# Masked cross attention on one core: masks as one 128-row product per bank, and a work order of its own

## What is computed

```python
def _L1_xattn_ref(q, k, v, mask, Wq, bq, Wk, bk, Wv, bv, Wo, bo):
    ...
    scale = 1.0 / jnp.sqrt(jnp.float32(dh))
    scores = jnp.einsum('hbsd,hbtd->hbst', qh, kh) * scale
    scores = jnp.where(mask == 0, jnp.float32(-1000000000.0), scores)
    attn = jax.nn.softmax(scores, axis=-1)
    out = jnp.einsum('hbst,hbtd->hbsd', attn, vh)
    out = out.transpose(1, 2, 0, 3).reshape(b, s, d)
    return out @ Wo.T + bo
x = x + jnp.tanh(g_xattn[1]) * _L1_xattn_ref(_layernorm(x, axis=-1), ctx_1024, ctx_1024, mask_SxS2_ik0, ...)
```

## Time and profile before

| what | us |
|---|---|
| median of 3 runs | 3282.59 |
| lowest, highest | 3279.39, 3283.39 |
| the profiled execution's own time | 3312.22 |
| its span, first to last instruction | 3310.4 |
| TensorE busy, share of the span | 2888.8 (87%) |
| VectorE busy | 2030.2 (61%) |
| ScalarE busy | 1995.5 (60%) |
| GpSimd busy | 1581.2 (48%) |
| granted TensorE clock, mean | 0.927 |

### The profile page before, as it was taken

How to read it: one execution, slowest core, us unless ns; L and a number is a source line. 1 busy time by engine, 2 the same in 40 slices (tenths; PEclk the granted TensorE clock), 3 DMA queues, 4 the chain that set the end, 5 groups by cost and what they waited for, 6 DMA issues and landing times. The chain is left out here.

```text
span 3310.4 us, 76280 instructions
## 1 busy us (share of the span) xinstructions
PE 2888.8 (87%) x27986; PEld 1847.8 (56%) x27986; DVE 2030.2 (61%) x3872; ACT 1995.5 (60%) x5960; POOL 1581.2 (48%) x1845
## 2 busy tenths in 40 slices
PE   4896998899889988998899879987999988996896
PEld 1554776467647664666477647763555543552452
DVE  3665886588658865886588758874333323665573
ACT  3345887588758885888488848883122233455343
POOL 0524885488638863887288728870311100420430
PEclk8798999999999999999999999999588899899798
DMA  2001001000010001000100010001000000000000
GB/s 92 1 2 45 16 18 40 17 18 18 20 36 18 18 15 42 18 18 15 41 17 18 16 40 18 18 16 53 1 1 1 1 1 0 1 2 0 1 2 13
DMA packets 35866, 60.31 MB, mean 18 GB/s; under 512 B 7184, under 2 KB 32656, under 8 KB 33552
## 3 DMA queue, kind: packets, MB, share of 16 engines
q1 hardware_dynamic: 35472, 55.15, 5.2%
HBM read 28.91 MB, written 1.05 MB: 9 GB/s over the span
## 5 line engine op out<-in xcount | busy, mean ns | idle before, releaser
L994 POOL TENSOR_TENSOR l_qk<-l_ta,l_tb 128x256 f32<-128x256 f32 x768 | 539.9, 735 | 113.4 <-DVE l_tb L1048 113.4
L617 POOL TENSOR_SCALAR qmr<-q_all,cf 128x256 fp32r<-128x256 f32 x128 | 116.0, 925 | 847.6 <-SPq L447 410.8
L649 DVE TENSOR_REDUCE mrow<-ring 128x2 f32<-128x512 f32 x512 | 328.2, 684 | 304.6 <-PE ring L491 290.8
L1010 POOL TENSOR_TENSOR l_qk<-l_qk,l_rn 128x512 f32<-128x512 f32 x384 | 392.7, 1044 | 217.0 <-DVE l_rn L1070 217.0
L602 ACT ACTIVATE pt<-st 128x512 f32<-128x512 f32 x384 | 210.6, 599 | 423.5 <-PE st L519 423.5
L915 ACT ACTIVATE l_pr<-st,l_mn 128x128 f32<-128x128 f32 x1152 | 407.5, 382 | 38.1 <-DVE l_mn L1036 38.1
L1001 POOL TENSOR_TENSOR l_pr<-l_pr,l_rs 128x512 f32<-128x512 f32 x384 | 391.9, 1043 | 42.5 <-DVE l_rs L1060 42.5
L1052 DVE TENSOR_REDUCE l_n<-l_sq 128x8 f32<-128x512 f32 x384 | 262.8, 686 | 177.8 <-ACT l_sq L924 175.6
L513 PE MATMUL st<-qm,k_all 32*128 32x512 f32 x1024 | 338.0, 691 | 0.0
L491 PE MATMUL ring<-ktr,qmr 32*128 32x256 f32 x1024 | 246.2, 403 | 14.3 <-POOL qmr L617 11.8
L915 ACT ACTIVATION_READ_ACCUMULATOR l_pr<-st,l_mn 128x1 f32 x1152 | 255.1, 221 | 0.0
(11 more groups left out here) (237 smaller groups left out, 6795.0 us busy)
## 6 DMA issues: line engine op xcount, KB each, us to landing
l_vm<-l_v SPq DMA_DIRECT2D x192, 96.0 KB, 2.0
l_wa<-in_wa SPq DMA_DIRECT2D x7, 2048.0 KB, 9.1
l_vm<-l_v SPq DMA_DIRECT2D x192, 32.0 KB, 1.9
l_wf<-in_wf SPq DMA_DIRECT2D x6, 580.5 KB, 4.6
w<-in_w SPq DMA_DIRECT2D x1, 2752.0 KB, 15.5
cf<-in_cf SPq DMA_DIRECT2D x1, 1253.0 KB, 7.4
x<-in_xT SPq DMA_DIRECT2D x1, 1024.0 KB, 4.8
ctxT<-in_ctxT SPq DMA_DIRECT2D x1, 1024.0 KB, 9.4
```

Of the source, the lines that this page charges most:

```text
L649: dve.tensor_reduce(mrow[b % 2][:, t, j, 2 * p:2 * p + 2], bank_of(f"R{r}").rearrange("p (h k) -> p h k", h=2), AX.X, ALU.max).then_inc(ri ...
L994: ins = pool.tensor_tensor(halves[0][:, :, x], halves[1][:, :, x], halves[2][:, :, 1 - x], ALU.add)
L1010: pool.tensor_tensor(part, part, t.rn[:, :, 4 * x:4 * x + 4].unsqueeze(3).broadcast_to([P, 2, 4, LHD]), ALU.mult).then_inc(qk_normed, 1)
```

## The change

- The mask is held as `mask2_q` and `mask2_k`: 128 mask rows on 128 partitions, two tiles of them, a quarter of the bytes. `add_mask` is one product of all 128 rows with the unit matrix over the 512 columns of a bank. The table of shifted unit matrices goes away.
- An item of scores is split in three: open (waits for its bank and, in the masked layer, adds the mask), add (the products of 32 rows), and for S subtract the maxima.
- Items of S and R that follow each other in the period form a run. In the masked layer a run first opens all its items, then adds all, then subtracts the maxima of all its S. In the other layers each item is a part of its own, in the old order.
- The masked layer has an order of its own, `MASKED_PERIOD`: four runs of four S with two or three R, four runs of one or two R, and between them the value quarters in pairs. Q0 to Q7 are in the batch itself, q8 to q15 in the next. Its first 20 row items go in runs of three.
- The ring plan is made for each layer's period.

```diff
-def project(g, l, q_all, k_all, mask4, tmp):
+def project(g, l, q_all, k_all, mask2, tmp):
...
-        ints = [tmp(n, [P, 4, 2, SEQ], I32) for n in ("mask_q", "mask_k")] if l == 1 else []
+        ints = [tmp(n, [P, 2, SEQ], I32) for n in ("mask_q", "mask_k")] if l == 1 else []
...
-                    for src, dst in zip(ints, mask4):
-                        dve.tensor_scalar(dst[:, :, :, :], src[:, :, :, :], 0.0, MASKED, ALU.is_equal, ALU.mult)
+                    for src, dst in zip(ints, mask2):
+                        dve.tensor_scalar(dst[:, :, :], src[:, :, :], 0.0, MASKED, ALU.is_equal, ALU.mult)
...
 PERIOD = ("q4 q5 q6 q7 R0 R1 S0 R2 S1 S2 S3 q8 R3 R4 q9 q10 q11 S4 S5 R5 R6 R7 S6 S7 q12 q13 q14 q15 V S8 R8 R9 "
           "S9 S10 S11 R10 Q0 Q1 R11 R12 Q2 Q3 O T S12 R13 S13 S14 S15 R14 R15").split()
+MASKED_PERIOD = ("S0 S1 S2 S3 R0 R1 R2 q8 q9 R3 q10 q11 S4 S5 S6 S7 R4 R5 R6 q12 q13 R7 q14 q15 V "
+                 "S8 S9 S10 S11 R8 R9 Q0 Q1 R10 R11 O Q2 Q3 S12 S13 S14 S15 R12 R13 T Q4 Q5 R14 R15 Q6 Q7").split()
...
+def runs_of(period):
+
+    runs = []
+    for item in period:
+        if item[0] in "SR" and runs and runs[-1][0][0] in "SR":
+            runs[-1].append(item)
+        else:
+            runs.append([item])
+    return runs
...
-            def add_mask(bank, rows, table):
-
-                for c in range(4):
-                    at = B_AT["shift"] + 96 - 32 * c
-                    pe.matmul(bank.rearrange("p (h k) -> p h k", h=2), g.cb[rows, at:at + P],
-                              table[rows, c, :].unsqueeze(1).broadcast_to([32, 2, SEQ]),
-                              start=c == 0, stop=False, skip_group_check=True)
+            def add_mask(bank, table):
+
+                pe.matmul(bank.rearrange("p (h k) -> p h k", h=2), g.b("ident"),
+                          table.unsqueeze(1).broadcast_to([P, 2, SEQ]), start=True, stop=False, skip_group_check=True)
...
+            def run_of_scores(b, items):
+
+                items = [(i[0], int(i[1:]) if i[0] == "S" else row_item(b, i)) for i in items]
+                items = [(kind, n) for kind, n in items if kind == "S" or n < 16 * NB]
+                for part in ([items] if l == 1 else [[i] for i in items]):
+                    for kind, n in part:
+                        if kind == "S":
+                            open_scores(b, n)
+                        else:
+                            open_rows(n)
+                    for kind, n in part:
+                        if kind == "S":
+                            add_scores(b, n)
+                        else:
+                            add_rows(n)
+                    for kind, n in part:
+                        if kind == "S":
+                            subtract_maxima(b, n)
...
+            size = 3 if l == 1 else 1
+            for start, end in ((0, 17), (17, 16 + ROWS_AHEAD)):
+                if start:
+                    turn_maxima(0)
+                for r in range(start, end, size):
+                    for x in range(r, min(r + size, end)):
+                        open_rows(x)
+                    for x in range(r, min(r + size, end)):
+                        add_rows(x)
```

More of the change, by code:

```diff
@@ L405, in row_item, with cross_attention @@
     return 16 * (b + 1) + ROWS_AHEAD + int(item[1:])
-RING_ORDER, RING_AT, RING_DVE = ring_plan()
-def cross_attention(g, l, q_all, k_all, mask4, tmp):
+RING_PLANS = [ring_plan(MASKED_PERIOD if l == 1 else PERIOD) for l in range(4)]
+def runs_of(period):
+    runs = []
+    for item in period:
+        if item[0] in "SR" and runs and runs[-1][0][0] in "SR":
[3 more added lines that the diff above has]
+    return runs
+def cross_attention(g, l, q_all, k_all, mask2, tmp):
     nc = g.nc
@@ L433, in cross_attention @@
     first = l * NB
-    ring0, ring0_dve = l * len(RING_ORDER), l * RING_DVE[-1]
+    period = MASKED_PERIOD if l == 1 else PERIOD
+    order, order_at, order_dve = RING_PLANS[l]
+    ring0 = sum(len(plan[0]) for plan in RING_PLANS[:l])
+    ring0_dve = sum(plan[2][-1] for plan in RING_PLANS[:l])
     has_bias = l in (1, 3)
@@ L438, in bank_of @@
     def bank_of(name):
[L439 removed]
+        return ring[:, order_at[name] % 3, :]
     def filled_at(name):
[L442 removed]
+        return ring0 + order_at[name] + 1
     def read_at(name):
[L445 removed]
+        return ring0_dve + order_dve[order_at[name]] + 1
     with nc.Block() as block:
@@ L450, in take_bank @@
             def take_bank(name):
-                if RING_AT[name] >= 3:
-                    old = RING_ORDER[RING_AT[name] - 3]
+                if order_at[name] >= 3:
+                    old = order[order_at[name] - 3]
                     if old[0] == "V":
@@ L482, in row_scores @@
                 bank = take_bank(f"R{r}")
-                rows = slice(32 * j, 32 * j + 32)
+                p, t, j = score_item(r % 16)
+                j = (j + 2) % 4
                 if l == 1:
-                    add_mask(bank, rows, mask4[0][:, :, t, :])
+                    add_mask(bank, mask2[0][:, t, :])
                 if l == 2:
+                    rows = slice(32 * j, 32 * j + 32)
                     pe.matmul(bank.rearrange("p (h k) -> p h k", h=2), g.b("selq")[rows],
@@ L489, in row_scores, with add_rows @@
                               start=True, stop=False, skip_group_check=True)
+            def add_rows(r):
+                b = r // 16
+                p, t, j = score_item(r % 16)
+                j = (j + 2) % 4
+                rows, bank = slice(32 * j, 32 * j + 32), bank_of(f"R{r}")
                 for x in range(2):
@@ L502, in turn_maxima, with open_scores, add_scores, subtract_maxima @@
                 mm.then_inc(ring_filled, 1)
-            def scores(b, n):
+            def open_scores(b, n):
                 p, kc, j = score_item(n)
-                item = 16 * (first + b) + n
+                if n == 0:
+                    pe.wait_ge(q_masked, first + b + 1)
                 if 16 * b + n >= 4:
-                    pe.wait_ge(probs_ready, item - 3)
-                rows, bank = slice(32 * j, 32 * j + 32), st[:, j, :]
-                at = b * SEQ + kc * P
+                    pe.wait_ge(probs_ready, 16 * (first + b) + n - 3)
                 if l == 1:
-                    add_mask(bank, rows, mask4[1][:, :, kc, :])
-                pe.matmul(bank, k_all[rows, at:at + P], qm[b % 2][rows, 2 * p:2 * p + 2, :].rearrange("p h q -> p (h q)"),
+                    add_mask(st[:, j, :], mask2[1][:, kc, :])
+            def add_scores(b, n):
+                p, kc, j = score_item(n)
+                rows, at = slice(32 * j, 32 * j + 32), b * SEQ + kc * P
+                pe.matmul(st[:, j, :], k_all[rows, at:at + P], qm[b % 2][rows, 2 * p:2 * p + 2, :].rearrange("p h q -> p (h q)"),
                           start=l != 1, stop=False, skip_group_check=True)
+            def subtract_maxima(b, n):
+                p, kc, j = score_item(n)
+                rows = slice(32 * j, 32 * j + 32)
                 if n == 0:
@@ L550, in _ @@
             pe.wait_ge(keys_r, 2 * l + 1)
[L551 to L555, removed]
-            for b in range(NB):
[L557 to L564, removed]
+            size = 3 if l == 1 else 1
[7 more added lines that the diff above has]
+                        add_rows(x)
+            for b in range(NB):
+                for run in runs_of(period):
+                    kind, n = run[0][0], int(run[0][1:] or 0)
+                    if kind in "SR":
+                        run_of_scores(b, run)
                     if kind == "Q":
@@ L574, in _ @@
                         project_back(b - 1)
-            for n in LATE:
+            for n in (int(item[1:]) for item in period if item[0] == "q"):
                 sum_values(NB - 1, n)
@@ L692, in _ @@
             for b in range(NB):
-                for item in PERIOD:
+                for item in period:
                     if item[0] == "R" and row_item(b, item) < 16 * NB:
```

22 lines of the change are left out of this document (8 added, 14 removed).

## The result

The median is 3150.67 us (3148.39 to 3153.18, four runs) against 3282.99 us (3279.39 to 3313.35, four runs): a ratio of 0.956, 95% interval 0.952 to 0.960. Faster, as forecast, and inside the range of 3115 to 3178; 12.7 us above the forecast of 3138. The profiled execution took 3153.18 us, its span is 3151.4: 159 us shorter than the profiled execution of before, while the medians differ by 132. Why these two differ is the first thing to explain.

A forecast was written before the change was run, and what follows sets the result against it. Masked cross attention taken as bound by TensorE alone, 178 us of it at half clock. Stage 169.8 + 12 + 10 + 37 + 6.5 + 3.7 = 239.0 against 383.4; with conversions 146.0 saved, median 3138, range 3115 to 3178.

The forecast's parts named there:

- Change of shape 0.10: TensorE going from 128-row masks to 32-row scores: 0.10 us each, eight runs a period, 0.8 us a batch.
- Period 25.8: Steady masked batch: 18.36 + 7.0 masks + 0.8 shape changes - 0.6 score runs + 0.2 value blocks; bounds 24.8 and 28.5.
- Waits of the new order: Masked-stage waits for banks, probabilities and maxima costed at nothing; 2 us a batch if the 0.8 us cover fails.
- First rows: First 20 rows of the masked stage, in threes: first S at about 30 us, 12 us more than the fourth layer.
- First batch: First masked batch, partly at the lower clock: 10 us above the fourth layer instead of 7.4.
- Conversions: Two mask conversions before the masked stage, at a quarter of the size: 1.6 us saved.
- The step from profile to median: Profiled execution 29.6 us above the median: spread evenly, median 3138; all in the masked stage, 3168.
- Rival A: Masked stage: clock still falls in turn, 0.50 for 31 us in each 89; 40 us more, 3178; chance 0.08.
- E: Better: clock rises in the first rows already and the period is 24.8; 15 us less, 3123; chance 0.07.
- B: Masked batches: waits or changes of shape cost more, 28.5 us a batch plus 2 us waits; 33 us, 3171; chance 0.12.
- C: Slower than before: clock at 0.50 for the whole masked stage, 430 us instead of 383, so 3328; chance 0.02.
- D: Mask products were hidden under other row groups, so the change doesn't do what it says; hardly any room.

The follow-up runs named there:

- third experiment: New kernel with the four 32-row mask products put back, new order and runs kept: 3169 us, ratio 0.962, a batch of 27.3 us.
- the product alone: One 128-row mask product a bank, but order of before and item by item, in the first rows too: 3524 us, ratio 1.071.
- the order alone: third experiment's kernel (four 32-row masks, new order) item by item instead of in runs: 3344 us, ratio 1.012.
- fourth experiment: New kernel with only the order undone: 128-row mask products and runs in the order of before; 3137.85 us, ratio 0.953, a batch of 23.6 us.
- eighth experiment: fourth experiment's kernel with runs grouped in all four cross attentions, not only the masked one: 3168 us.
- sixth experiment: third experiment's kernel with the last of four mask products made twice, five an item: 3222 us, a batch of 33.4 us.
- third execution: Kernel before, unchanged, profiled once more: 3280.5 us, its masked stage 359.1 us, against 3312.2 and 383.4 us in the first profile.

## Why grouping lets 32-row masks run side by side

In the kernel before, the masks of S8 start at 2509.66 and are alone; the first mask of the next item, on another row group, starts just behind the first score product of S8, its fifth instruction (timeline of TensorE):

```profile
2510.32 0.37 PE L463 MATMUL st<-mask_k,cb 32*128 32x512 bf16 x1
2510.54 0.59 PE L513 MATMUL st<-qm,k_all 32*128 32x512 f32 x1
2510.55 0.38 PE L463 MATMUL ring<-mask_q,cb 32*128 32x512 bf16 x1
```

S8 has eight instructions on its row group (four masks, two score passes, two maxima). A row item has six, and behind it the next item starts with its third: the third mask of R8 and the first of R9 start together.

```profile
2510.99 0.39 PE L463 MATMUL ring<-mask_q,cb 32*128 32x512 bf16 x2
```

With runs, each item has four mask products before the next item's. There a window that opens 0.04 us after the first mask and closes 0.15 later already finds four of them running, one of each of S0 to S3 (in the trace each of them has its own item's wait in front), and 16 masks take 0.91 us (2434.81 to 2435.72):

```profile
2434.81 0.42 PE L478 MATMUL st<-mask_k,cb 32*128 32x512 bf16 x4
...
2434.81 1.07 PE L478 MATMUL st<-mask_k,cb 32*128 32x512 bf16 x16
2435.72 0.84 PE L478 MATMUL ring<-mask_q,cb 32*128 32x512 bf16 x9
```

So products of a later item start before earlier ones of the item ahead, as long as only three of those still wait behind the one that runs. In S8's case that holds from the fifth instruction on, in R8's from the third. The test was a fifth mask product an item (the last one made twice; the output is the same):

```diff
-            def add_mask(bank, rows, table, chunks=range(4)):
+            def add_mask(bank, rows, table, chunks=(0, 1, 2, 3, 3)):
```

> The third experiment's kernel (new order, runs, 32-row masks) with the last of the four mask products made twice, so five for each item. Theory: TensorE holds three products waiting behind the one that runs for each row group, and the next product in the program can't pass once one has to wait outside; so with four mask products the first masks of S0 to S3 start 13 ns apart (seen), with five they start 0.22 us apart, and the batch grows from 27.3 to about 33 us (2.6 for the products, 3 for the stagger). Rival (the row groups run freely, whatever their number): the first masks still start together and the batch is 29.9 us.

A window from 0.01 to 0.16 us behind the first mask finds one mask started, not four. The first masks of S0 to S3 start 0.23 us apart, each just behind the second mask of the item ahead, which then has three waiting. The row masks start 1.56 us after the first mask instead of 0.91:

```profile
2443.44 0.38 PE L478 MATMUL st<-mask_k,cb 32*128 32x512 bf16 x1
...
2443.44 1.74 PE L478 MATMUL st<-mask_k,cb 32*128 32x512 bf16 x19
2445.00 0.37 PE L478 MATMUL ring<-mask_q,cb 32*128 32x512 bf16 x1
```

The batch is 33.4 us (33 expected by the theory, 29.9 by the rival); the kernel 3222 us. The theory holds in this number too. What the limit counts (products, or products with their weight loads) no run separates.

## The price of a 128-row product, and the clock

The new kernel makes its 128-row mask product four times for each bank here; the output is the same.

```diff
-                pe.matmul(bank.rearrange("p (h k) -> p h k", h=2), g.b("ident"),
-                          table.unsqueeze(1).broadcast_to([P, 2, SEQ]), start=True, stop=False, skip_group_check=True)
+                for c in range(4):
+                    pe.matmul(bank.rearrange("p (h k) -> p h k", h=2), g.b("ident"),
+                              table.unsqueeze(1).broadcast_to([P, 2, SEQ]), start=c == 0, stop=False, skip_group_check=True)
```

> The new kernel with its 128-row mask product made four times for each bank (the same output). It gives the price of a 128-row product without more changes of shape: 96 more a batch. Theory 1: 0.216 us each, 25.2 + 20.7 = 45.9 us a batch at full clock, and the granted clock stays at 1.00 although as many mask products of 512 columns run in a row as before; kernel 3315 to 3335. Theory 2 (long chains of mask products go with the slow clock, whatever their rows): 31 us stretches at 0.50 return, kernel above 3370.

A batch is 45.9 us: (45.91 - 25.19) / 96 = 0.216 us a product, as a 32-row one. The Trainium skill gives the same rule, in TensorE: Matmul & The Clock Gate, Why this matters for your kernels: a single matmul of 32 rows takes the time of one of 128; here the run shows it for 512 bf16 columns. The kernel took 3302 us (3300 to 3311), 13 below the expected 3315 to 3335. In the profiled execution, of 3311 us, the clock rose during the first rows already, which the estimate didn't have:

```profile
2328.00:2680.00 352.00, 345.86 (x2673) 156.40 (x2672) 106.09 (x171) 65.06 (x134) 59.73 (x67) 1.00 0.00 1
```

As many mask products in a row as before, and no stretch at the lower level. With the table above: behind the first S the clock was low for long in the three kernels of the table whose masked items go one by one through one row group at a time. It fell again and again before (0.77 to 0.83 over the stage) and with the product alone (0.60), and in the profiled execution of the order alone it stayed low for 117 us behind the first S. In the kernels with runs, and in this one, it was up within 4 us of the first S and stayed up to the last microsecond of the stage (the first rows ran at 0.56 in the new kernel). What exactly lets it fall isn't shown. That TensorE is busy without a gap doesn't keep it up.

## Looking for a better kernel

**Runs in all four attentions**, the old order in all of them as in the fourth experiment:

```diff
-                for part in ([items] if l == 1 else [[i] for i in items]):
+                for part in [items]:
```

> The fourth experiment's kernel (order of before, 128-row masks, runs) with runs grouped in all four cross attentions. Theory 1: the fourth experiment's 23.63 us a batch less 32 x 0.216 of masks and 6 x 0.093 of changes is 16.2 us, 2.1 below the fourth layer's 18.36, so grouping the score items helps without masks as well: 3 layers x 7 batches x 2.1 = 45 us, kernel about 3093. Theory 2 (without masks between them ScalarE and VectorE release the banks too late, and TensorE waits for them instead): periods of 17.5 us or more and less than 20 us gained, kernel above 3118.

Measured 3168 us, 31 above the fourth experiment; the second theory's "above 3118" holds. A batch of the fourth layer is 19.1 us instead of 18.36: the first theory falls. Without masks an S item has only four instructions, so its neighbours overlapped already, and a run that opens everything first now waits where masks had covered it. The longest of these waits stands behind T, 1.30 us until VectorE has read the turned maxima; behind V it is 1.3 us up to the run's scores where V takes 0.65 in the earlier trace rows:

```profile
3001.46 0.71 PE L482 MATMUL ring<-w,ctxT 128*128 128x128 f32 x4
3002.79 0.66 PE L533 MATMUL st<-qm,k_all 32*128 32x512 f32 x1 [0.63 <-ACT vpad L635]
...
3009.03 0.66 PE L533 MATMUL st<-qm,k_all 32*128 32x512 f32 x1 [1.30 <-DVE mt L705]
```

**New order in the three other layers**, the masked one as in the fourth experiment; with runs and item by item:

```diff
-RING_PLANS = [ring_plan(MASKED_PERIOD if l == 1 else PERIOD) for l in range(4)]
+RING_PLANS = [ring_plan(PERIOD if l == 1 else MASKED_PERIOD) for l in range(4)]
...
-    period = MASKED_PERIOD if l == 1 else PERIOD
+    period = PERIOD if l == 1 else MASKED_PERIOD
```

The one with runs also has the edit of the eighth experiment above.

> Masked layer as in the fourth experiment (old order, runs, 128-row masks, 23.6 us a batch); the other three cross attentions in the new order with runs. In the eighth experiment grouping cost them 0.7 us a batch, because a run opened right behind V waited for banks (0.9 us in a row); the new order puts four value quarters and a short run between two long ones. Theory: 25.2 - 6.9 (masks) - 0.74 (changes) = 17.5 us a batch there, 0.8 below 18.36, kernel about 3122. Rival: without the masks' 0.9 us of cover the waits stay and a batch is 18.4 or more, kernel 3138 or more.

> As the run before, but in the three layers without this mask the items aren't grouped, only their order is the new one. An S item has four instructions there, which by the sixth experiment doesn't hold back the next, so the items should overlap without runs and release their banks earlier. Theory: between 17.5 and 18.4 us a batch, kernel 3120 to 3140, no worse than the grouped form by more than 5 us. Rival (the row items behind four S items in a row are late): above 18.4 and above 3140.

With runs 3150.6 us, a batch of 18.45: the theory of 17.5 falls, and the rival's 18.4 is met. Item by item 3134.4 us (3132.6 to 3134.9), ratio to before 0.952 (0.947 to 0.957), a batch of 17.9 us in the first and the fourth layer and 19.1 for 19.0 in the third. The theory's two ranges hold, but for the third layer, which gained nothing. It is the fastest of all, by 3 us over the fourth experiment, which was run in another comparison; both lie 13 to 16 us below the new kernel.

## Why the prediction was right, and where not

- Bound by TensorE: right; after the change too, as the waits show.
- The mask product at 0.22 us: right (0.216). Change of shape 0.10: right (0.09). Period 25.8: measured 25.2; the long runs came out shorter than the 1.7 us taken for each (2432.35 to 2433.89 is 1.54), and V goes over into the masks without a change of shape, which I had not counted off. (The forecast's lower bound of 24.8 is 25.0 by its own terms.)
- Waits of the new order costed at nothing: right, no matmul waits for probabilities in 100 us.
- First rows: right to a tenth. The first S comes 29.9 us after the start (30 forecast), 12.0 above the fourth layer.
- First batch: wrong by 8 us. From the first S to the second batch's first S it is 22.0 us, 2.0 above the fourth layer's 20.0, where I put 10. I had the clock rise 15 us after the first S; it rose at it.
- Batches 1 to 5: 34.2 us for 37. Batch 6: 5.0 for 6.5. Last batch: 1.8 for 3.7. Together the stage is 224.7 for 239.0.
- Conversions: each step on VectorE fell from 1.13 to 0.33 us, the 1.6 expected. The stage started 1.0 us later nevertheless: the projection ahead of it, from its first product on, had a granted clock of 0.65 and then 0.81 in its two halves, against 0.77 and 0.91 before.
- The step from profile to median failed. I spread 29.6 us evenly, though the stage's windows showed a clock that alternates, and named the other case (all in this stage, 3168) only as a bound. By the third execution three quarters of them lie in the stage, and the new kernel, whose clock doesn't fall there, has no such step: its profiled execution is 2.5 us above its median, where I took off 28.2. That the forecast of 3138 is so near is luck, for two errors offset: the gain in the profiled execution was put 13.0 us too low (146.0 for 159.0, the stage's terms above), and the step to the median 25.7 too large. Together they make the 12.7 by which the forecast was too low.
- The reasoning on what the change replaces was wrong in its cause. I priced 128 products at 19.2 us a batch and took the 128-row product as what removes them. In runs the same products cost some 8.7 us a batch (an estimate: 24.9 less 16.2, which is the fourth experiment's 23.6 less its masks and changes), because four row groups then share them; one by one, the 128-row product alone loses 240 us. The sum came out since the grouped stream was costed step by step, and the grouping stood in it as a mere condition.
- The forecast took 0.2% as what a measurement can tell. The kernel before alone spreads over 1% from execution to execution (3277 to 3314 us).
- Rival A (the clock still falls): didn't come; E came in part: the clock rose at the end of the first rows, not in them, and the period is 25.2, not 24.8. B and C didn't come. D was right to ask whether 32-row masks can hide under one another and wrong to look only at the kernel before.

## What to carry to other kernels

In these kernels products on separate row groups overlap only if what the program places between them on one group is short: put the first products of several items side by side before the longer chains. Count changes between 128-row and 32-row products at 0.09 us each, so group them too. Try the old order before writing a new one. Where the granted clock alternates in a profile, take a second profile before scaling a gain to the median.

## What the runs showed of the hardware that was not expected

- In these traces a row group takes the running product and three more; a fourth that would have to wait holds back every later product in the program. Items with four, five, six and eight instructions in a row on one group all fit this. Four mask products an item: 27.3 us a batch; five: 33.4.
- Products start out of program order across row groups: with runs and four mask products an item (third experiment), the first masks of four items start within 0.04 us though three masks of each stand between them.
- The clock fell to 0.50 with TensorE busy all the time (before), and the same kernel drew 0.77, 0.81 or 0.83 over the stage in three executions. Four runs of the new kernel, which has no such stretches behind its first S, lie within 5 us.
